# TensorE and VectorE read 44 of 59 expert numbers into registers ahead of the block loop, the other 15 in the first blocks

## The reference, cut to what matters

```python
x = x + relu(attention(layernorm(x), ctx, ctx, mask) @ wo_w.T + wo_b)     # x: 8 x 112 x 256, ctx: 8 x 375 x 256, 16 heads
xf = layernorm(x).reshape(896, 256)
scores = softmax(xf @ gw + gb)                                           # 32 experts in 8 groups
weights, indices = top 4 experts of the 4 best groups                    # per token
for e in range(32):                                                      # only the chosen ones count
    h = silu(xf @ w1[e] + b1[e]) * (xf @ w3[e] + b3[e])                  # 256 -> 128
    y += cw[:, e] * (h @ w2[e] + b2[e])                                  # 128 -> 256
x = x + y + silu(xf @ sw1 + sb1) * (xf @ sw3 + sb3) @ sw2 + sb2
```

## Time and profile before

| what | value |
|---|---|
| device time, median of 3 runs | 406.81 us (405.06 to 408.76) |
| the profiled execution | 404.81 us, of which the span of its instructions is 403.0 us |
| busy, share of the span | PE 73%, DVE 55%, ACT 36%, POOL 38% |
| mean granted TensorE clock | 0.883 of full speed |
| attention and gate, up to the last TensorE work of the gate | 0 to 195.9 us |
| scatter on GpSimd | 186.1 to 227.4 us |
| block loop on TensorE, first to last instruction | 231.0 to 354.5 us |
| gather and sum | 357.6 to 403 us |

### The profile page before, as it was taken

The page is one execution under the profiler, slowest core; times in us unless marked ns, Lnnn a source line. Parts: engine busy times, 40 slices in busy tenths (PEclk is TensorE's granted clock), DMA queues, the critical chain, the costliest instruction groups (busy, mean ns, idle before and its releaser), DMA issues.

```text
span 403.0 us, 7155 instructions
## 1 busy us (share of the span) xinstructions
PE 293.2 (73%) x2283; PEld 201.4 (50%) x2283; DVE 222.4 (55%) x696; ACT 147.1 (36%) x403; POOL 152.5 (38%) x153
## 2 busy tenths in 40 slices
PE   8999999999999975989400099899989899910000
PEld 3466666666666754656200076576766566600000
DVE  2878777677776946678600035555545455513333
ACT  2376676666766661310000033434343344400000
POOL 4566666666666721004777400000000000037773
PEclk9999999999999995999855579999999999965555
DMA  6519688596682001920222314444344344323332
GB/s 160 171 44 297 195 289 228 171 334 215 218 261 111 2 2 64 291 63 23 91 91 91 109 52 132 141 121 142 121 132 130 107 142 125 114 86 114 116 117 74
DMA packets 39420, 55.31 MB, mean 137 GB/s; under 512 B 4173, under 2 KB 30810, under 8 KB 38874
## 3 DMA queue, kind: packets, MB, share of 16 engines
q1 hardware_dynamic: 36314, 47.52, 37.9%
q0 software_dynamic: 3072, 7.34, 6.1%
HBM read 34.79 MB, written 20.05 MB: 136 GB/s over the span
## 4 chain that ended last, share of the span: by engine, by line
PE 27%; POOL 15%; issue 7%; DMA 6%; DVE 5%; POOLq 0%; ACT 0%; SPq 0%; DVEq 0%
PE ps L830 14%; POOL expert_rows L742 8%; POOL b L748 7%; PE ps L845 6%; DMA xg<-expert_rows 5%; PE ps L822 3%; PE ps L839 1%; PE ps L766 1%; PE ps L758 1%; DMA b<-expert_out,slots 1%; DMA expert_rows<-normed,slots 1%; DVE x L1054 0%; PE ps L796 0%; PE ps L791 0%; DMA expert_out<-y_sb 0%
## 5 line engine op out<-in xcount | busy, mean ns | idle before, releaser
L261 POOL TENSOR_SCALAR z<-z,zmax 112x375 f32<-112x375 f32 x64 | 78.5, 1238 | 53.9 <-DVE zmax L521 53.9
L748 POOL DMA_INDIRECT b<-expert_out,slots x32 | 29.9, 934 | 139.6 <-DMA expert_out<-y_sb 130.2
L521 DVE CUSTOM_DVE_ANT_0 z<-ps,mask_sb 112x375 f32<-112x375 f32 x128 | 62.5, 545 | 28.2 <-PE ps L340 28.1
L830 PE MATMUL ps<-w,xgT 128*128 x236 | 67.6, 410 | 6.4 <-ACT xgT L887 4.9
L1041 DVE TENSOR_TENSOR hb<-ps,b 128x256 f32<-128x256 f32 x59 | 25.1, 425 | 83.6 <-PE ps L830 83.6
L449 ACT ACTIVATE pT<-ps 125x336 f32<-125x336 f32 x128 | 50.7, 448 | 38.2 <-PE ps L317 37.7
L317 PE MATMUL ps<-ident,z 112*125 112x112 f32 x384 | 56.6, 284 | 0.2 <-ACT pT L449 0.2
L830 PEld LDWEIGHTS ps<-w,xgT 128*128 128x128 f32 x236 | 41.6, 194 | 29.4 <-issue 25.7
L317 PEld LDWEIGHTS ps<-ident,z 112*125 112x125 f32 x384 | 47.4, 188 | 15.4 <-ACT pT L449 7.3
L822 PE MATMUL ps<-ident,xg 128*128 128x128 f32 x118 | 23.5, 283 | 38.4 <-DMA xg<-expert_rows 38.4
L742 POOL DMA_INDIRECT expert_rows<-normed,slots x32 | 31.9, 997 | 36.5 <-DVE slots L1007 27.1
(11 more groups left out here) (142 smaller groups left out, 339.9 us busy)
## 6 DMA issues: line engine op xcount, KB each, us to landing
xg<-expert_rows SPq DMA_DIRECT2D x59, 128.0 KB, 2.2
expert_out<-y_sb SPq DMA_DIRECT2D x59, 128.0 KB, 1.7
expert_rows<-zero SPq DMA_DIRECT2D x14, 512.0 KB, 9.1
w2s<-in_L_ffn_w SPq DMA_DIRECT2D x2, 2048.0 KB, 10.1
b<-in_L_ffn_b SPq DMA_DIRECT2D x2, 2048.0 KB, 12.7
ctx_sb<-in_ctx SPq DMA_DIRECT2D x8, 375.0 KB
mask_sb<-in_mask_Bx1xSxS_ff SPq DMA_DIRECT2D x8, 164.1 KB, 2.4
out_x<-x SPq DMA_DIRECT2D x8, 112.0 KB, 2.0
```

Of the source, the lines that this page charges most:

```text
L261: pool.tensor_scalar(z[:, n % RING, :], z[:, n % RING, :], zmax[:, n % RING:n % RING + 1], None, ALU.subtract).then_inc(by_pool, 1)
L521: nc.vector.tensor_tensor_reduce(out=z[:, n % RING, :], in0=ps[0:S, S_BANK + j, 0:SK], in1=mask_sb[:, b % 2, :], scale=-1.0 if j in ACT_HE ...
L748: pool.indirect_dma_start(rows[:, TOPK * b + r, :], None, ys, bass.IndirectOffsetOnAxis(ap=slots[:, b, r:r + 1], axis=0)).then_inc(rows_in ...
L830: ins = nc.tensor.matmul(ps[:, U_BANKS[j % 2], 0:2 * INTER], xgT[:, j % 4, k, :], w13[:, k, bass.ds(own[j], 1), :].rearrange("p o c -> p ( ...
```

## The change

The two lists of `value_load` are split. Right after `table_ok`, and before its other waits, TensorE reads the numbers of blocks 0 to 43 into 44 registers (line 850 of the new file); the other 15 are read one by one behind `down(0)` to `down(14)`, each ahead of the `up` of the next iteration (line 868), into what the finished blocks' numbers leave free. VectorE reads 44 as well, behind its sums for the gate (line 1039 of the new file), and the other 15 ahead of `hb(1)` to `hb(15)` (line 1044). From iteration 18 on TensorE reads none, and from iteration 16 on VectorE. The number of reads is 59 on each engine, as before. No other engine's list changes.

```diff
+            HELD = 44
...
-                own = {}
-
...
-
                 pe.wait_ge(table_ok, 1)
+                own = {j: pe.value_load(owner_i[0:1, j:j + 1], min_val=0, max_val=E - 1) for j in range(HELD)}
+
                 pe.wait_ge(acc_ok, B)
                 pe.wait_ge(cwT_ok, NCH)
                 pe.wait_ge(weights_in, 16 * 6)
...
                 turn_rows(1)
                 for j in range(NBLK + 2):
                     if j < NBLK:
-                        own[j] = pe.value_load(owner_i[0:1, j:j + 1], min_val=0, max_val=E - 1)
                         up(j)
...
                         turn_rows(j + 2)
                     if j >= 2:
                         down(j - 2)
+                    if j >= 2 and j - 2 + HELD < NBLK:
+
+                        own[j - 2 + HELD] = pe.value_load(owner_i[0:1, j - 2 + HELD:j - 1 + HELD], min_val=0, max_val=E - 1)
...
                 dve.wait_ge(table_ok, 1)
+                own = {j: dve.value_load(owner_i[0:1, j:j + 1], min_val=0, max_val=E - 1) for j in range(HELD)}
                 dve.wait_ge(scale_in, 16 * 2)
                 for j in range(NBLK + 3):
                     if j < NBLK:
-                        e = dve.value_load(owner_i[0:1, j:j + 1], min_val=0, max_val=E - 1)
+                        if j >= 1 and j - 1 + HELD < NBLK:
+                            own[j - 1 + HELD] = dve.value_load(owner_i[0:1, j - 1 + HELD:j + HELD], min_val=0, max_val=E - 1)
                         dve.wait_ge(up_done, j + 1)
                         TT(hb[:, j % 2, :], ps[:, U_BANKS[j % 2], 0:2 * INTER],
-                           b13[:, bass.ds(e, 1), :].rearrange("p o c -> p (o c)"), ALU.add).then_inc(biased, 1)
+                           b13[:, bass.ds(own[j], 1), :].rearrange("p o c -> p (o c)"), ALU.add).then_inc(biased, 1)
```

## The result

The change made the kernel slower, by 1.5%: 414.62 us (median of 4 runs, 410.72 to 416.33) against 407.32 us before (4 runs). The ratio is 1.0153, with a 95% interval of 1.0098 to 1.0209. Forecast were 398.8 us and a range of 394.0 to 404.5. The profiled execution after took 415.27 us, its span 413.4, against 404.81 and 403.0.

What follows compares the result with a forecast made beforehand. TensorE bounds the block loop, with gaps from reading the expert number ahead of `up`. Ordinary blocks 6.6 us, late loads 1.1, start 0.3, reads in front 0: 406.8 - 8.0 = 398.8 us, range 394.0 to 404.5.

Steps and rivals of the forecast that it cites:

- The reads in front ... cost 0, hidden by the scatter: Ahead of the block loop: 44 reads per engine at 0.7 us, 30.8 us, done at 226.1, before the first turn.
- The end of my range: Ahead of the loop: reads at 0.9 us each would start the loop 3.9 us late, 402.7 us; chance 0.03.
- reads cost much more in a series: Rival, ahead of the loop: at twice 0.8 us per read TensorE is 34.7 us late, 433 us; chance 0.01.
- point of decision: Ahead of the loop: beyond 0.81 us per read, (231.0 - 195.3) / 44, the loop starts late.
- No read here is near that: Argument against reads costing more in a series: the longest TENSOR_LOAD of both engines is 548 ns.
- Slower: the reads hold up the scatter: Rival, ahead of the loop: VectorE's reads slow 24 scatters by 0.9 us each, loop 21.6 us later, 420 us; chance 0.03.
- The transfer ... 1.74 to 1.78 us each: Blocks 17 to 58: store, load and turn of rows take 5.22 to 5.33 us over three blocks and set the pace.
- the first of the three cycles of the prediction: Blocks 17 to 58: the array alone, 1.62 us per block, expected not to be the slowest cycle.
- Blocks 0 to 17 ... 0.3 us: Start of the loop: up(0) to up(2) lose their reads in the half-clock stretch, a gain of 0.3 us.
- Late loads: Blocks 17 to 58: four late loads, 4.5 us over the median together; catching up after them gains 1.1 us.
- The sum: Whole kernel: a gain of 8.0 us, from a median of 406.8 to 398.8 us.

## Why the prediction was wrong, point by point

- **"The reads in front ... cost 0, hidden by the scatter": this step failed.** It measured 14.8 us. I had taken the price of a read, 0.7 us, from rows in which no scatter ran, and the only read beside the scatter was a single one. The price holds without the scatter (0.65 us, 44 times); beside it, from the 15th to the 24th read, it was 3.2 us. The end of my range (0.9 us each, 3.9 us late) was no bound, as it came from rows of the same undisturbed kind. The rival "reads cost much more in a series" had the right place, and its point of decision was right too, 0.81 us per read against a measured mean of (248.6 - 194.0) / 44 = 1.24; I gave it 0.01. The chance was far too low, since no row showed a dense list of sequencer instructions beside the scatter, and "No read here is near that" was lack of evidence, not evidence. The length of a TENSOR_LOAD, by which I had weighed it, was the wrong thing to look at: any instruction of the sequencer is held.
- **"Slower: the reads hold up the scatter": no.** The later scatters last 0.94 to 0.95 us as before. Only the first two last longer (1.86 and 1.80 us), with the reads and without; in the kernel that holds the scatter back, where VectorE does nothing beside it, they take 1.16 and 0.94. The effect goes the other way, from the scatter to the sequencers. The Trainium skill, page "SBUF — State Buffer", box on the "DVE blocks DMA" trap, describes GpSimd as the one that is locked out; no run here shows that for these reads.
- **"The transfer ... 1.74 to 1.78 us each": right.** 1.73 to 1.82 us in the chain; 76.3 us for the 41 blocks against 75.7 forecast, 74.2, 75.1 and 77.2 in the three other kernels in which TensorE's reads are out of the way. The move of the store shows that it was this cycle: with a block more of lead the array's 1.62 is reached, which was the first of the three cycles of the prediction.
- **"Blocks 0 to 17 ... 0.3 us": right in size, by luck.** It was 0.5 us to `up(17)` (35.8 us from the first turn instead of 36.3). But the half clock reached 5.7 us into the loop before and 3.7 us after, although I had said that nothing in the change moves it; and the kernel with the 132 semaphore instructions, whose loop has all its reads, needs 35.4 us with 3.6 us of half clock. So nothing shows that the 0.5 us come from the reads.
- **Late loads.** Over each of the longest landings in the changed loop (3.34, 3.87, 3.42 and 3.55 us in the chain from 285 us on) the DMA queues again carry one packet of kind "instruction". The decision to count them stands; that the packet is what delays the load is read from the two coming together, and no run takes it away. With the store moved five loads still landed after 2.9 to 3.9 us, each over such a packet, and TensorE waited 0.9 us in all: the lead hides them. The rule of the Trainium skill, page "Runtime: NRT & Kernel Launch", section "Instruction fetch mechanics", that a fetch is mostly hidden, agrees with that kernel, whose loads have slack, and not with the kernel before, where four loads were 4.5 us late in all and the moved store by itself, which gives them a block of lead, took 4.9 us off.
- **The sum.** -8.0 us forecast; -7.6 in the loop and its start, +0.2 at the end, +14.8 in front, so +7.4 against the measured +7.3.

What stays open is what fills up. Every run here was made with its instructions recorded, so I can't tell whether the slow stretch belongs to the chip's work or to the recording of it. The Trainium skill, page "NOTIFIC — the notification-queue block", section "Overflow: three behaviours, one of which stalls the engine", says that the block that writes such records holds the producers back when its own pipeline is full. That would fit two sequencers held at once, whatever their instruction, and the dependence on their number; no run here separates it from another shared path. One sign points the same way: in the slow stretch some TENSOR_LOADs stand on record with 3 ns, where none outside it is under 292 ns, and the instructions of both engines start in steps of about 0.70 us (204.69, 205.40, 206.12, 206.82 us). A start that is written down late would look like this; it is a sign and no proof. If it is the recording, the reads in front would be hidden in a run without it.

## What to carry to other kernels

A stretch in which an engine idles is not free for anything: before moving work there, look in the trace for that kind of work beside what runs there now, and give "never seen together" a real chance of going wrong. Work that the sequencer has to do fits better behind an instruction that keeps the array busy than in front of the loop: reading one number ahead behind `up` needs one register more instead of 44 and gave 2.8%. And where two limits lie within 0.2 us per block of each other, remove both: 4.9 and 6.2 us alone, 16.0 us together.

## What the runs showed of the hardware that was not expected

- While GpSimd's 32 indirect DMAs ran, the sequencers of TensorE and VectorE passed a semaphore instruction in 0.15 us and a read of three instructions in 0.65 us until 11.6 to 23.2 us after the first DMA, and then took up to 1.4 us per instruction, until some 6 us after the last DMA started (229.65, end of the slow stretch 235.6 us). TENSOR_LOAD, FUSED_REGOPS, SEQ_ASSERT and EVENT_SEMAPHORE were held alike; GpSimd's own pace of 1.25 us per scatter didn't change.
- A read without the check of its bounds took 0.42 us of the sequencer in a series (44 starts from 191.1 to 209.1 us) instead of 0.65, but its use in the loop cost more: 1.99 us per block against 1.86.
